# Token-shift mixes moved from VectorE to ScalarE and GpSimd, with a new table of steps, in a Mamba layer between two feed-forward blocks

## The chip, the cores and the metric

One core of one Trainium2 chip. The metric is the device time of one execution in microseconds, the median of the runs. Engines as the profile names them: PE is TensorE (PEld its weight loads), DVE is VectorE, ACT is ScalarE, POOL is GpSimd, SP is SyncE, which issues the DMAs.

## The reference

The input is 4 sequences of 2048 tokens with 512 features, fp32. Half a feed-forward block is added, then a Mamba block with its residual, then the same feed-forward block again:

```python
def ffn(x):                                     # W_r, W_k, W_v are 512 x 512, mu_r and mu_k have 512
    x_prev = concatenate([zeros, x[:, :-1]], axis=1)
    xr = mu_r * x + (1.0 - mu_r) * x_prev
    xk = mu_k * x + (1.0 - mu_k) * x_prev
    r = sigmoid(xr @ W_r.T)
    k_act = square(relu(xk @ W_k.T))
    return r * (k_act @ W_v.T)

def mamba(x):                                   # 1024 inner channels, 16 states
    xs, z = split(layernorm(x, ln_w, ln_b) @ W_in.T)
    xc = silu(b_conv + causal_conv(xs, W_conv, taps=4))
    dt_low, B, C = split(xc @ W_xproj.T)
    delta = softplus(dt_low @ W_dt.T + b_dt)
    h = exp(delta * A) * h + delta * B * xc     # a scan over the tokens
    y = (h * C).sum(states) + D_skip * xc
    return (y * silu(z)) @ W_out.T + x

x = x + 0.5 * ffn(layernorm(x))
x = x + mamba(layernorm(x))
x = x + 0.5 * ffn(layernorm(x))
```

The change is in `xr` and `xk`.

## The kernel before

The tokens are cut into 16 chunks of 512, four of each sequence in turn. Features lie on the 128 partitions for what is multiplied, tokens for what is normalised. A chunk's scan is 64 **steps**: 4 quarters of the channels (256 each, two tiles of 128) by 16 states. In each step ScalarE makes the decay (`make_decay`, lines 886 to 889: two exponentials and a zero between them), GpSimd the product of u and B (`product`, lines 1298 and 1302), VectorE scans (line 1091) and multiplies by C into g (`weigh`, line 1099), TensorE adds g up by transposing it into the accumulator y_acc (`sum_g`, line 567), ScalarE saves the last state (`save`, line 895), and SyncE loads the rows of B and C for later steps. Two decay buffers, two g buffers and four buffers of products tie the engines: ScalarE makes decay s when state s-2 is saved, which needs the multiply of step s-2; GpSimd makes product s when multiply s-4 is done.

One iteration of the loop has the 64 steps of one chunk. All other work is spread over them: the first feed-forward block and the Mamba front (input projection, convolution, x projection) of the next chunk ("front"), and the output projection and second feed-forward block of the chunk before ("back"). The step in which each piece stands is in a table of numbers written into the kernel (`TURN` to `BANK`); each engine's program goes through the 64 steps and issues in each, after its part of the scan, what the table puts there, in a fixed order of pieces. Engines run their programs in order and wait on semaphores, so a piece that waits holds up everything behind it, the decays and products of later steps too. Iterations -2 and -1 and 16 and 17 have no scan: they are the head and the tail of the program.

A feed-forward block in the order of its pieces, with the lines of the profile: ScalarE normalises rows (691), TensorE turns them (458), ScalarE copies the columns (`ffn_columns`, 708, and `ffn_lead`, 715 and 717) into `col`, which is one token longer than the chunk. Then the **mixes**: ScalarE scales the previous token by 1 - mu into `mix_k` (`ffn_before_k`, 732) and into the other mix (`ffn_before_r`, 748; it lies in `xn_col` for the first block, in `xin` for the second), and VectorE adds mu times the token itself:

```python
dve.scalar_tensor_tensor(out=mix_k[:, ct, :], in0=col[:, ct, 1:W + 1], scalar=vec[:, 1, ct:ct + 1],
                         in1=mix_k[:, ct, :], op0=ALU.mult, op1=ALU.add)      # ffn_mix_k, 1014; ffn_mix_r is 1019
```

There are 16 of these per chunk: four feature tiles, k and r, two blocks. TensorE then makes k (`ffn_k`, 472, which waits for all four k mixes), r (`ffn_r`, 483) and v (`ffn_v`, 494); ScalarE makes relu and square in `col` (756, 758) and tanh (762); VectorE gates (1026) and GpSimd adds to the residual (1287). Groups of four matmuls of 512 columns are the unit on TensorE. Others that are spoken of: the output projection (596), the x projection (531, in two halves), after which ScalarE writes `xdbl` (820), softplus with its two table loads (837, 845), the convolution (802, 1037), its silu on VectorE (1043), `make_u` (1276), and `add_zeros` (575), matmuls of a zero tile into y_acc that change nothing in it, put at the steps in `ZEROS`.

## Time and profile before

| | us |
|---|---|
| median of 3 runs | 4891.49 |
| lowest, highest | 4890.23, 4892.57 |
| span of the profiled execution | 4888.0 |
| first scan begins | 153.6 |
| last scan begins | 4779.8 |
| mean granted clock of TensorE | 0.971 |

The span is the profiled execution's own time from its first to its last instruction; the runs' median is 3.5 us longer. The program has 58,099 instructions. A busy time is the union of an engine's instructions; each instruction's time overlaps the next one's by a little, so an engine without gaps shows a step from start to start that is shorter than the sum of the durations. TensorE's matmul ends are modelled.

### The profile page before, as it was taken

The page shows a single profiled execution, that of the slowest core. Times are in us where ns is not written, and L with a number is a line of the kernel's source. Part 1 is how long each engine was busy: PE and PEld are TensorE (multiplying, and loading weights), DVE is VectorE, ACT ScalarE, POOL GpSimd, SP SyncE. Part 2 cuts the span into 40 slices and gives each one's busy share as a digit, 9 for nine tenths or more (in the row PEclk, how much of TensorE's full clock was granted, in tenths as well). Part 3 has the DMA queues.
Part 4 walks back from the last instruction along what each step waited for, and adds up shares of the span by engine and source line. Part 5 has one row for each costly group of instructions (what it writes and reads, how often), then busy time and mean ns, then how long its engine had stood idle before and what let it go on. Part 6 is the DMA issues. An engine that isn't in the chain of part 4 may idle for free.

```text
span 4888.0 us, 58099 instructions
## 1 busy us (share of the span) xinstructions
PE 4296.9 (88%) x16896; PEld 2382.9 (49%) x16896; DVE 4488.3 (92%) x3650; ACT 2900.1 (59%) x6355; POOL 3196.4 (65%) x3328
## 2 busy tenths in 40 slices
PE   6777989898999989989898899989999898999787
PEld 2444545454554545545454454545545454554443
DVE  2799999999999999999999999999999999999992
ACT  2555656666666566656666665666656666665452
POOL 1666767576676767767576676767667576776770
PEclk9888999999999999999999999999999999999798
DMA  2445555454554555555555554555555565655451
GB/s 82 141 135 180 172 171 185 163 183 162 189 169 151 189 168 186 172 173 185 158 174 163 186 172 152 190 179 176 172 185 173 155 180 156 190 170 153 167 164 62
DMA packets 423053, 810.71 MB, mean 166 GB/s; under 512 B 41264, under 2 KB 41264, under 8 KB 418640
## 3 DMA queue, kind: packets, MB, share of 16 engines
q1 hardware_dynamic: 422736, 807.00, 52.1%
q8 instruction: 136, 2.23, 0.2%
q14 instruction: 181, 1.48, 0.1%
HBM read 772.25 MB, written 34.60 MB: 165 GB/s over the span
## 4 chain that ended last, share of the span: by engine, by line
DVE 38%; PE 29%; issue 16%; ACT 7%; POOL 6%; DMA 3%; DVEq 0%; SPq 0%; POOLq 0%; ACTq 0%
DVE decay L1091 19%; DVE g L1099 10%; PE y_acc L567 6%; PE mm L494 5%; PE mm L483 5%; POOL dbx L1298 4%; PE mm L472 4%; DVE xc L1037 3%; DMA c_all<-bc_scratch 2%; PE mm L531 2%; PE mm L509 2%; PE mm L519 2%; DVE xc L1043 1%; ACT decay L889 1%; POOL xout L1287 1%
## 5 line engine op out<-in xcount | busy, mean ns | idle before, releaser
L1298 POOL TENSOR_TENSOR dbx<-u,b_all 128x1024 f32<-128x1024 f32 x1024 | 2414.2, 2358 | 902.6 <-DVE g L1099 901.7
L1091 DVE TENSOR_TENSOR_SCAN decay<-decay,state,dbx 128x1024 f32<-128x1024 f32 x1024 | 2405.4, 2349 | 172.4 <-ACT decay L889 157.6
L567 PE MATMUL y_acc<-ident,g 128*128 128x128 f32 x8192 | 1124.2, 283 | 372.5 <-DVE g L1099 370.6
L567 PEld LDWEIGHTS y_acc<-ident,g 128*128 128x128 f32 x8192 | 947.4, 144 | 939.1 <-DVE g L1099 713.2
L1099 DVE TENSOR_TENSOR g<-decay,c_all 128x1024 f32<-128x1024 f32 x1024 | 1244.3, 1215 | 10.0 <-DMA c_all<-bc_scratch 1.1
L886 ACT ACTIVATE decay<-delta,neg_a 128x512 f32<-128x512 f32 x1024 | 708.7, 692 | 36.9
L889 ACT ACTIVATE decay<-delta,neg_a 128x511 f32<-128x511 f32 x1024 | 686.9, 671 | 0.0
L895 ACT ACTIVATE state<-decay 128x2 f32<-128x2 f32 x1024 | 166.9, 163 | 508.6 <-DVE g L1099 506.1
L494 PE MATMUL mm<-wbuf_c,col 128*128 128x512 f32 x1024 | 460.9, 594 | 2.1 <-ACT col L758 1.3
L1037 DVE SCALAR_TENSOR_TENSOR xc<-mm,conv_sb,xc 128x509 f32<-128x509 f32 (+2 forms) x384 | 285.3, 743 | 47.0 <-ACT xs_last L804 35.7
L1302 POOL TENSOR_TENSOR dbx<-dbx,carry 128x1 f32<-128x1 f32 x1024 | 274.2, 268 | 80.3
L494 PEld LDWEIGHTS mm<-wbuf_c,col 128*128 128x128 f32 x1024 | 185.0, 190 | 192.0 <-issue 186.5
L802 ACT ACTIVATE xc<-mm,evec,conv_sb 128x512 f32<-128x512 f32 x128 | 99.5, 777 | 257.0 <-PE mm L509 222.9
L762 ACT ACTIVATE rows<-mm 128x512 f32<-128x512 f32 x128 | 76.2, 595 | 294.2 <-PE mm L483 294.2
L472 PE MATMUL mm<-mix_k,wbuf_c 128*128 128x512 f32 x512 | 232.7, 598 | 4.5 <-DVE mix_k L1014 4.4
L509 PE MATMUL mm<-xn_col,wbuf_d 128*128 128x512 f32 x512 | 235.2, 603 | 1.3 <-ACT xn_col L789 1.0
L483 PE MATMUL mm<-wbuf_d,xin 128*128 128x512 f32 x512 | 231.8, 596 | 4.4 <-DVE xin L1019 4.4
L596 PE MATMUL mm<-wbuf_a,gate 128*128 128x512 f32 x512 | 233.1, 598 | 2.1 <-issue 1.2
L472 PE MATMUL mm<-mix_k,wbuf_b 128*128 128x512 f32 x512 | 233.0, 599 | 1.7 <-DVE mix_k L1014 1.7
L509 PE MATMUL mm<-xn_col,wbuf_a 128*128 128x512 f32 x512 | 232.7, 598 | 1.4 <-DVE xc L1037 1.4
L519 PE MATMUL mm<-xn_col,wbuf_b 128*128 128x512 f32 x512 | 231.2, 594 | 0.0
L519 PE MATMUL mm<-xn_col,wbuf_c 128*128 128x512 f32 x512 | 230.6, 593 | 0.0
(100 smaller groups left out, 5107.4 us busy)
## 6 DMA issues: line engine op xcount, KB each, us to landing
b_all<-bc_scratch SPq DMA_DIRECT2D x1024, 256.0 KB, 3.4
c_all<-bc_scratch SPq DMA_DIRECT2D x1024, 256.0 KB, 3.6
wbuf_d<-in_w_r SPq DMA_DIRECT2D x32, 1024.0 KB, 7.5
wbuf_c<-in_w_v SPq DMA_DIRECT2D x32, 1024.0 KB, 7.3
xin<-in_x SPq DMA_DIRECT2D x16, 1024.0 KB, 6.8
wbuf_c<-in_w_k SPq DMA_DIRECT2D x16, 1024.0 KB, 6.7
wbuf_d<-in_w_in SPq DMA_DIRECT2D x16, 1024.0 KB, 5.8
wbuf_a<-in_w_in SPq DMA_DIRECT2D x16, 1024.0 KB, 8.0
```

The lines of the kernel that those rows point to most:

```text
L472: last = pe.matmul(bank(it, f"f{i}k{j}"), wk[:, ct, j * P:(j + 1) * P], mix_k[:, ct, :], start=ct == 0, stop=ct == CT - 1)
L483: last = pe.matmul(bank(it, f"f{i}r{tb}"), mix_r[:, ct, tb * P:(tb + 1) * P], wr[:, ct, :], start=ct == 0, stop=ct == CT - 1)
L494: last = pe.matmul(bank(it, f"f{i}v{tb}"), col[:, ct, tb * P:(tb + 1) * P], wv[:, ct, :], start=ct == 0, stop=ct == CT - 1)
L509: last = pe.matmul(bank(it, f"xs{e}"), win[:, ct, e % 4 * P:(e % 4 + 1) * P], xn_col[:, slot, ct, :], start=ct == 0, stop=ct == CT - 1)
L519: last = pe.matmul(bank(it, f"z{e}"), win[:, ct, e % 4 * P:(e % 4 + 1) * P], xn_col[:, slot, ct, :], start=ct == 0, stop=ct == CT - 1)
L567: last = pe.matmul(y_acc[:, tb, j * P:(j + 1) * P], g[:, s % PAIRS, j, tb * P:(tb + 1) * P], ident[:, :], start=n == 0 and j == 0 and tb % ...
L886: act.activation(d[:, 0, :], delta[:, q % 2, 0, :], ACT.Exp, scale=neg_a[:, e, n:n + 1]).then_inc(decay_done, 1)
L889: act.activation(d[:, 1, 1:W], delta[:, q % 2, 1, 1:W], ACT.Exp, scale=neg_a[:, e + 1, n:n + 1]).then_inc(decay_done, 1)
L1037: dve.scalar_tensor_tensor(out=o, in0=src[:, 0:W - late], scalar=conv_sb[:, e, q:q + 1], in1=o, op0=ALU.mult, op1=ALU.add).then_inc(m_dve. ...
L1091: dve.tensor_tensor_scan(d, d, flat(dbx[:, s % DBX, :, :]), state[:, batch, s, 0:1], ALU.mult, ALU.add).then_inc(scan_done, 1)
L1099: dve.tensor_tensor(g[:, s % PAIRS, :, :], decay[:, s % PAIRS, :, :], c_all[:, s % CRING, :].unsqueeze(1).broadcast_to([P, QT, W]), ALU.mu ...
L1298: pool.tensor_tensor(dbx[:, s % DBX, :, :], u[:, q % 2, :, :], b_all[:, s % BRING, :].unsqueeze(1).broadcast_to([P, QT, W]), ALU.mult).the ...
```

## The change

VectorE's 16 mixes per chunk are gone. ScalarE, which scaled the previous token, scales the token itself as well, by mu, into a free tile (`now`): `rows[0]` for the k mix of the first block, `rows[1]` for the r mix of the second, and `col` in place for the mix that comes last in its block. GpSimd adds the two tiles. In the second block r comes before k on ScalarE. TensorE and ScalarE wait for GpSimd's adds where they waited for VectorE's mixes, and tanh waits for an add too, since it overwrites the tile. The table of steps is new. Of its 40 or so lines these are the ones that matter here (first block or front ahead, second behind):

```diff
-        MM_K = ((5, 7, 8, 9), (46, 47, 50, 51))
+        MM_K = ((5, 7, 8, 9), (46, 48, 49, 52))
-        ZEROS = {2: 2, 31: 2, 39: 2, 30: 1, 53: 1}
+        ZEROS = {31: 1}
-        COLUMNS = ((1, 1, 2, 2), (36, 36, 36, 36))
+        COLUMNS = ((1, 2, 2, 3), (36, 36, 36, 36))
-        BEFORE_K = ((3, 3, 5, 5), (39, 39, 40, 40))
+        BEFORE_K = ((3, 3, 4, 5), (39, 39, 40, 43))
-        BEFORE_R = ((6, 7, 7, 7), (37, 37, 38, 38))
+        BEFORE_R = ((3, 5, 7, 8), (36, 37, 37, 38))
-        XROWS = 51
+        XROWS = 52
-        MIX_K = ((3, 4, 5, 5), (42, 43, 45, 46))
+        MIX_K = ((3, 4, 5, 6), (41, 42, 42, 49))
-        MIX_R = ((6, 7, 7, 8), (38, 39, 40, 40))
+        MIX_R = ((4, 6, 9, 9), (38, 39, 39, 40))
-        CSILU = (33, 34, 40, 42, 43, 45, 48, 48)
+        CSILU = (34, 36, 43, 43, 48, 48, 48, 49)
-        MAKE_U = (-8, 9, 27, 38)
+        MAKE_U = (-2, 8, 28, 37)
```

Besides, in the table: `MM_R` of the first block goes from (10, 10, 12, 13) to (10, 10, 11, 13), `XPROJ` from (49, 50) to (48, 50), `RELU` of the second block from (49, 50, 53, 53) to (49, 50, 51, 54), the loads `wxs1` from 26 to 31 and `wo0` from 48 to 51; `MM_V` is the same. Other numbers move by a step or two. The code:

```diff
@@ -203,15 +204,15 @@
                      *[(COLUMNS[i][n], f"xn{n}" + " lead last" * (n == 3)) for n in range(4)],
                      *[(RELU[i][n], f"rel{n} sq{n}") for n in range(4)],
                      *[(TANH[i][n], f"th{n}") for n in range(4)],
-                     *[(BEFORE_K[i][n], f"pk{n}") for n in range(4)],
-                     *[(BEFORE_R[i][n], f"pr{n}") for n in range(4)])) for i in range(2)]
+                     *[(q[i][n], f"p{r}{n} a{r}{n}")
+                       for q, r in ((BEFORE_K, "k"), (BEFORE_R, "r"))[::(1, -1)[i]] for n in range(4)])) for i in range(2)]
         f_dve = [Marks(sem(f"ffn{i}_dve"), in_order(
                      *[(STATS[i][n] - 64 * (2 - i), f"st{n}") for n in range(4)],
                      (MEANS[i] - 64 * (2 - i), "mv0 mv1 mv2 mv3"),
+                     *[(GATE[i][n], f"g{n}") for n in range(4)])) for i in range(2)]
+        f_pool = [Marks(sem(f"ffn{i}_pool"), ["v"] + newton + ["mean", "shift"] + in_order(
                      *[(MIX_K[i][n], f"xk{n}") for n in range(4)],
-                     *[(MIX_R[i][n], f"xr{n}") for n in range(4)],
-                     *[(GATE[i][n], f"g{n}") for n in range(4)])) for i in range(2)]
-        f_pool = [Marks(sem(f"ffn{i}_pool"), ["v"] + newton + ["mean", "shift", "o0", "o1", "o2", "o3"])
+                     *[(MIX_R[i][n], f"xr{n}") for n in range(4)]) + ["o0", "o1", "o2", "o3"])
                   for i in range(2)]
         m_pe = Marks(sem("mamba_pe"), in_order(*[(MTURN[n], f"T{n}") for n in range(4)],
                                                *[(XS[e], f"xs{e}") for e in range(ET)], (XPROJ[1], "xp")))
@@ -283,6 +284,10 @@
                 if 0 <= it + off < NCH and home(it, name) == mine:
                     return marks.sem, marks.at(it + off, emptied)
             return None
+
+        def now(i, part, ct):
+
+            return rows[i][:, ct, :] if i == part else col[:, ct, 1:W + 1]
 
         def flat(t):
             return t.rearrange("p a b -> p (a b)")
@@ -463,7 +468,7 @@
                 turn_rows(it, f"f{i}T{ct}", rows[i], ct, f_pe[i])
 
             def ffn_k(it, i, k, j):
-                pe.wait_ge(f_dve[i].sem, f_dve[i].at(k, "xk3"))
+                pe.wait_ge(f_pool[i].sem, f_pool[i].at(k, "xk3"))
                 pe.wait_ge(wk_loaded[i], 16 * (k + 1))
                 if free := bank_free(it, f"f{i}k{j}"):
                     pe.wait_ge(*free)
@@ -474,7 +479,7 @@
                 last.then_inc(f_pe[i].sem, 1)
 
             def ffn_r(it, i, k, tb, mix_r):
-                pe.wait_ge(f_dve[i].sem, f_dve[i].at(k, "xr3"))
+                pe.wait_ge(f_pool[i].sem, f_pool[i].at(k, "xr3"))
                 pe.wait_ge(wr_loaded[i], 16 * (k + 1))
                 if free := bank_free(it, f"f{i}r{tb}"):
                     pe.wait_ge(*free)
@@ -731,6 +736,12 @@
                         act.wait_ge(f_pe[1].sem, count)
                 act.activation(mix_k[:, ct, :], col[:, ct, 0:W], ACT.Copy,
                                scale=vec[:, 3, ct:ct + 1]).then_inc(f_act[i].sem, 1)
+                if i == 0:
+                    act.wait_ge(f_pe[0].sem, f_pe[0].at(k, "T3"))
+                else:
+                    act.wait_ge(f_act[1].sem, f_act[1].at(k, f"pk{ct}"))
+                act.activation(now(i, 0, ct), col[:, ct, 1:W + 1], ACT.Copy,
+                               scale=vec[:, 1, ct:ct + 1]).then_inc(f_act[i].sem, 1)
 
             def ffn_before_r(i, k, ct, mix_r, fronted=True):
 
@@ -747,11 +758,17 @@
                             act.wait_ge(f_pe[1].sem, count)
                 act.activation(mix_r[:, ct, :], col[:, ct, 0:W], ACT.Copy,
                                scale=vec[:, 2, ct:ct + 1]).then_inc(f_act[i].sem, 1)
+                if i == 1:
+                    act.wait_ge(f_pe[1].sem, f_pe[1].at(k, "T3"))
+                else:
+                    act.wait_ge(f_act[0].sem, f_act[0].at(k, f"pr{ct}"))
+                act.activation(now(i, 1, ct), col[:, ct, 1:W + 1], ACT.Copy,
+                               scale=vec[:, 0, ct:ct + 1]).then_inc(f_act[i].sem, 1)
 
             def ffn_relu2(i, k, j):
 
                 act.wait_ge(f_pe[i].sem, f_pe[i].at(k, f"k{j}"))
-                act.wait_ge(f_dve[i].sem, f_dve[i].at(k, (f"xr{j}", f"xk{j}")[i]))
+                act.wait_ge(f_pool[i].sem, f_pool[i].at(k, (f"xr{j}", f"xk{j}")[i]))
                 o = col[:, j, 0:W]
                 act.activation(o, bank(k - (1, -1)[i], f"f{i}k{j}"), ACT.Relu).then_inc(f_act[i].sem, 1)
                 act.wait_ge(f_act[i].sem, f_act[i].at(k, f"rel{j}"))
@@ -759,6 +776,7 @@
 
             def ffn_tanh(i, k, tb):
                 act.wait_ge(f_pe[i].sem, f_pe[i].at(k, f"r{tb}"))
+                act.wait_ge(f_pool[i].sem, f_pool[i].at(k, (f"xk{tb}", f"xr{tb}")[i]))
                 act.activation(rows[i][:, tb, :], bank(k - (1, -1)[i], f"f{i}r{tb}"), ACT.Tanh,
                                scale=0.5).then_inc(f_act[i].sem, 1)
 
@@ -962,10 +980,10 @@
                         for n in at(BEFORE_R[0], s):
                             ffn_before_r(0, f, n, xn_col[:, other, :, :])
                     if back:
+                        for n in at(BEFORE_R[1], s):
+                            ffn_before_r(1, b, n, xin, front)
                         for n in at(BEFORE_K[1], s):
                             ffn_before_k(1, b, n, front)
-                        for n in at(BEFORE_R[1], s):
-                            ffn_before_r(1, b, n, xin, front)
                     if front:
                         for e in at(CTANH, s):
                             conv_tanh(f, e)
@@ -1008,16 +1026,6 @@
                     dve.wait_ge(marks.sem, marks.at(k, f"st{tb}"))
                     dve.sem_inc(passed_dve, 1)
                     dve.bn_aggr(mv[q][:, tb, :], stats[q][:, tb, :]).then_inc(marks.sem, 1)
-
-            def ffn_mix_k(i, k, ct):
-                dve.wait_ge(f_act[i].sem, f_act[i].at(k, f"pk{ct}"))
-                dve.scalar_tensor_tensor(out=mix_k[:, ct, :], in0=col[:, ct, 1:W + 1], scalar=vec[:, 1, ct:ct + 1],
-                                         in1=mix_k[:, ct, :], op0=ALU.mult, op1=ALU.add).then_inc(f_dve[i].sem, 1)
-
-            def ffn_mix_r(i, k, ct, mix_r):
-                dve.wait_ge(f_act[i].sem, f_act[i].at(k, f"pr{ct}"))
-                dve.scalar_tensor_tensor(out=mix_r[:, ct, :], in0=col[:, ct, 1:W + 1], scalar=vec[:, 0, ct:ct + 1],
-                                         in1=mix_r[:, ct, :], op0=ALU.mult, op1=ALU.add).then_inc(f_dve[i].sem, 1)
 
             def ffn_gate(i, k, tb):
                 dve.wait_ge(f_pe[i].sem, f_pe[i].at(k, f"v{tb}"))
@@ -1108,16 +1116,6 @@
                     if scn:
                         scan(it, s, bt)
 
-                    if front:
-                        for n in at(MIX_K[0], s):
-                            ffn_mix_k(0, f, n)
-                        for n in at(MIX_R[0], s):
-                            ffn_mix_r(0, f, n, xn_col[:, other, :, :])
-                    if back:
-                        for n in at(MIX_K[1], s):
-                            ffn_mix_k(1, b, n)
-                        for n in at(MIX_R[1], s):
-                            ffn_mix_r(1, b, n, xin)
                     if front:
                         for e in at(CSILU, s):
                             conv_silu(f, e)
@@ -1281,6 +1279,14 @@
                 pool.tensor_tensor(carry[:, q % 2, :], carry[:, q % 2, :], state[:, batch, NS * q:NS * q + NS, 1],
                                    ALU.mult).then_inc(h_pool.sem, 1)
 
+            def ffn_mix_k(i, k, ct):
+                pool.wait_ge(f_act[i].sem, f_act[i].at(k, f"ak{ct}"))
+                pool.tensor_tensor(mix_k[:, ct, :], mix_k[:, ct, :], now(i, 0, ct), ALU.add).then_inc(f_pool[i].sem, 1)
+
+            def ffn_mix_r(i, k, ct, mix_r):
+                pool.wait_ge(f_act[i].sem, f_act[i].at(k, f"ar{ct}"))
+                pool.tensor_tensor(mix_r[:, ct, :], mix_r[:, ct, :], now(i, 1, ct), ALU.add).then_inc(f_pool[i].sem, 1)
+
             def ffn_add(i, k, tb):
                 pool.wait_ge(f_dve[i].sem, f_dve[i].at(k, f"g{tb}"))
                 o = (xin, xout)[i][:, tb, :]
@@ -1311,6 +1317,16 @@
                     if scn:
                         for q in at(MAKE_U, s):
                             make_u(it, q, bt)
+                    if front:
+                        for n in at(MIX_K[0], s):
+                            ffn_mix_k(0, f, n)
+                        for n in at(MIX_R[0], s):
+                            ffn_mix_r(0, f, n, xn_col[:, (bt + 1) % 2, :, :])
+                    if back:
+                        for n in at(MIX_K[1], s):
+                            ffn_mix_k(1, b, n)
+                        for n in at(MIX_R[1], s):
+                            ffn_mix_r(1, b, n, xin)
                     if front:
                         for n in at(FFN_ADD[0], s):
                             ffn_add(0, f, n)
```

How ScalarE's program changes in step 3 of a steady iteration (state and decay are the scan's, mix_k and xn_col the two mixes of the first block, col the columns). Before, from the state saved in step 3:

```order
L895 ACTIVATE state<-decay 128x2
L886 ACTIVATE decay<-delta,neg_a 128x512
L888 ACTIVATE decay<-zero 128x1
L889 ACTIVATE decay<-delta,neg_a 128x511
L732 ACTIVATE mix_k<-col,vec 128x512 x2
```

and now, from behind the decay of step 3 to the decay of step 4:

```order
L713 ACTIVATE col<-mm 128x512
L720 ACTIVATE col<-ffn_last0 128x4
L722 ACTIVATE ffn_last0<-col 128x4
L737 ACTIVATE mix_k<-col,vec 128x512
L743 ACTIVATE rows0<-col,vec 128x512
L737 ACTIVATE mix_k<-col,vec 128x512
L743 ACTIVATE rows0<-col,vec 128x512
L759 ACTIVATE xn_col<-col,vec 128x512
L765 ACTIVATE col<-col,vec 128x512
L913 ACTIVATE state<-decay 128x2
L904 ACTIVATE decay<-delta,neg_a 128x512
```

The last column copy and its two small ones came into step 3 from step 2, and two scaled copies have become six.

GpSimd's program in steps 3 to 6 of the same iteration (dbx are the products). Before, step after step alike:

```order
L1298 TENSOR_TENSOR dbx<-u,b_all 128x1024
L1302 TENSOR_TENSOR dbx<-dbx,carry 128x1
L1298 TENSOR_TENSOR dbx<-u,b_all 128x1024
L1302 TENSOR_TENSOR dbx<-dbx,carry 128x1
L1298 TENSOR_TENSOR dbx<-u,b_all 128x1024
```

and now:

```order
L1304 TENSOR_TENSOR dbx<-u,b_all 128x1024
L1308 TENSOR_TENSOR dbx<-dbx,carry 128x1
L1284 TENSOR_TENSOR mix_k<-mix_k,rows0 128x512
L1304 TENSOR_TENSOR dbx<-u,b_all 128x1024
L1308 TENSOR_TENSOR dbx<-dbx,carry 128x1
L1284 TENSOR_TENSOR mix_k<-mix_k,rows0 128x512
L1288 TENSOR_TENSOR xn_col<-xn_col,col 128x512
L1304 TENSOR_TENSOR dbx<-u,b_all 128x1024
L1308 TENSOR_TENSOR dbx<-dbx,carry 128x1
L1284 TENSOR_TENSOR mix_k<-mix_k,rows0 128x512
L1304 TENSOR_TENSOR dbx<-u,b_all 128x1024
L1308 TENSOR_TENSOR dbx<-dbx,carry 128x1
```

An add now stands between the products of each of these steps, and waits for ScalarE.

TensorE's program from the second k group of the second block (mix_k) to the last, with the x projection's halves (wx_sb) between. Before:

```order
L472 MATMUL mm<-mix_k,wbuf_b 128x512 x4
L567 MATMUL y_acc<-ident,g 128x128 x16
L531 MATMUL mm<-xc2,wx_sb 64x512 x4
L567 MATMUL y_acc<-ident,g 128x128 x8
L472 MATMUL mm<-mix_k,wbuf_b 128x512 x4
L531 MATMUL mm<-xc2,wx_sb 64x512 x4
L567 MATMUL y_acc<-ident,g 128x128 x8
L472 MATMUL mm<-mix_k,wbuf_b 128x512 x4
```

and now:

```order
L477 MATMUL mm<-mix_k,wbuf_b 128x512 x4
L536 MATMUL mm<-xc2,wx_sb 64x512 x4
L572 MATMUL y_acc<-ident,g 128x128 x8
L477 MATMUL mm<-mix_k,wbuf_b 128x512 x4
L572 MATMUL y_acc<-ident,g 128x128 x8
L536 MATMUL mm<-xc2,wx_sb 64x512 x4
L572 MATMUL y_acc<-ident,g 128x128 x16
L556 MATMUL y_acc<-ident,spare 128x128 x8
L477 MATMUL mm<-mix_k,wbuf_b 128x512 x4
```

Two sums of g now stand behind the second half of the x projection before the last k group; one stood there.

## Rows read from the trace of the kernel before

**Rows 1.** The page's engines: busy us (share of the span) and instructions.
```profile
PE 4296.9 (88%) x16896; PEld 2382.9 (49%) x16896; DVE 4488.3 (92%) x3650; ACT 2900.1 (59%) x6355; POOL 3196.4 (65%) x3328
```

**Rows 2.** Stretches: us; busy us (instructions) per engine; TensorE clock; DMA share, GB/s.
```profile
0.00:153.60 153.60, 93.44 (x212) 40.54 (x212) 39.64 (x70) 48.30 (x82) 27.69 (x88) 0.90 0.24 75
2191.70:2207.60 15.90, 10.43 (x64) 7.34 (x64) 15.83 (x13) 12.89 (x29) 10.55 (x8) 1.00 0.93 314
2207.60:2268.20 60.60, 59.54 (x227) 32.94 (x228) 56.67 (x40) 36.28 (x81) 42.20 (x32) 1.00 0.50 157
2351.70:2426.40 74.70, 65.03 (x244) 33.82 (x245) 74.12 (x63) 43.53 (x101) 41.81 (x35) 1.00 0.54 173
2426.40:2484.30 57.90, 53.50 (x212) 28.98 (x210) 52.95 (x46) 32.98 (x72) 43.36 (x48) 1.00 0.52 159
2191.70:2484.30 292.60, 264.00 (x1056) 145.87 (x1056) 280.31 (x230) 180.80 (x397) 199.74 (x207) 0.99 0.54 173
4527.00:4779.80 252.80, 198.28 (x834) 122.62 (x833) 240.86 (x166) 137.42 (x317) 172.55 (x148) 0.88 0.49 161
```

**Rows 3.** VectorE's timeline in steps 38 and 52: start, us, [idle before].
```profile
2363.28 0.92 DVE L1019 SCALAR_TENSOR_TENSOR xin<-col,vec,xin 128x512 f32<-128x512 f32 x1
2364.12 0.67 DVE L1048 SCALAR_TENSOR_TENSOR gate<-gate,mm 128x512 f32<-128x512 f32 x1
...
2434.51 2.36 DVE L1091 TENSOR_TENSOR_SCAN decay<-decay,state,dbx 128x1024 f32<-128x1024 f32 x1 [4.05 <-ACT decay L889]
```

**Rows 4.** Chain of waits, end of step 51: start, us, what.
```profile
2420.60 3.58 PE mm L531 x8
...
2425.20 3.44 PE mm L472 x8
2428.64 3.59 PE mm L531 x8
...
2432.25 0.69 ACT xdbl L820
...
2433.02 0.69 ACT decay L886
```

**Rows 5.** Groups by line and shape: busy us, mean ns of one, idle before.
```profile
L1014 DVE SCALAR_TENSOR_TENSOR mix_k<-col,vec,mix_k 128x512 f32<-128x512 f32 x128 | 113.2, 897 | 13.7 <-ACT mix_k L732 13.7
...
L1019 DVE SCALAR_TENSOR_TENSOR xn_col<-col,vec,xn_col 128x512 f32<-128x512 f32 x64 | 63.3, 1010 | 6.7 <-ACT xn_col L748 6.7
...
L1019 DVE SCALAR_TENSOR_TENSOR xin<-col,vec,xin 128x512 f32<-128x512 f32 x64 | 53.8, 862 | 13.6 <-ACT xin L748 13.6
...
L1287 POOL TENSOR_TENSOR xin<-xin,rows 128x512 f32<-128x512 f32 x64 | 81.4, 1271 | 167.2 <-DVE rows L1026 165.5
...
L575 PE MATMUL y_acc<-ident,zero 128*128 128x512 f32 x256 | 135.0, 643 | 0.0
```

**Rows 6.** ScalarE's timeline in steps 4 and 5.
```profile
2205.53 1.28 ACT L837 ACT_TABLE_LOAD   x1 [0.48 <-PE mm L543]
...
2209.68 0.15 ACT L895 ACTIVATE state<-decay 128x2 f32<-128x2 f32 x1
...
2211.20 1.32 ACT L732 ACTIVATE mix_k<-col,vec 128x512 f32<-128x512 f32 x2
```

**Rows 7.** TensorE's timeline in steps 2, 6, 8 and 50.
```profile
2200.71 1.88 PE L575 MATMUL y_acc<-ident,zero 128*128 128x512 f32 x4
...
2217.24 3.60 PE L472 MATMUL mm<-mix_k,wbuf_c 128*128 128x512 f32 x8
...
2227.11 1.09 PE L567 MATMUL y_acc<-ident,g 128*128 128x128 f32 x8 [0.96 <-DVE g L1099]
...
2419.51 1.09 PE L567 MATMUL y_acc<-ident,g 128*128 128x128 f32 x8 [1.31 <-DVE g L1099]
```

**Rows 8.** Durations of VectorE's k mixes and of its silus, ns min/median/max.
```profile
L1014 DVE SCALAR_TENSOR_TENSOR mix_k<-col,vec,mix_k x128: 736/910/1789, 31.2 to 4838.3; 128x512 f32<-128x512 f32 x128
...
L1043 DVE SCALAR_TENSOR_TENSOR xc<-rows,xc x128: 676/680/999, 110.8 to 4460.2; 128x512 f32<-128x512 f32 x128
```

57 lines of the change are left out of this document (29 added, 28 removed), and 6 rows, old and new, of the table BANK.

## Prediction

> **What bounds the kernel now.** I read the engines' shares first: VectorE is busy for 92% of the span, TensorE for 88% [rows 1]. Two engines are near their limit, so an average decides nothing, and I cut one steady iteration (the eighth, 292.6 us between the starts of its first scan and of the next iteration's) at the starts of steps 4, 18, 36 and 51. Head and last iteration stand beside it [rows 2]. Over the whole iteration ScalarE is busy 180.8 us and GpSimd 199.7, so neither is near. Fifteen iterations lie between 153.6 and 4527.0 us, 291.6 us each. The reader is to see two regimes. In steps 4 to 18 TensorE is busy 59.5 of 60.6 us and VectorE 56.7: TensorE sets the pace. In steps 36 to 51 VectorE is busy 74.1 of 74.7 us and TensorE 65.0: VectorE sets it [rows 2]. In steps 51 to 64 both have gaps, 4.4 us on TensorE and 5.0 on VectorE, most of the latter in one wait of 4.05 us for ScalarE's decay [rows 3]. The chain of waits tells whose wait that is: projection, up matmul, projection on TensorE back to back, then xdbl on ScalarE, then the decay queued behind it, then the scan [rows 4]. So from step 48 on the chain runs through TensorE as well.
>
> **What is removed from VectorE.** 256 mixes go: 113.2 + 63.3 + 53.8 = 230.3 us busy, 0.90 each [rows 5]. Instructions overlap a little: the mix at 2363.28 is followed at 2364.12 [rows 3], so one mix holds the engine 0.84 us. That is 13.4 us for the 16 of an iteration, of which a half belongs to each feed-forward block.
>
> The eight of the first block stand in steps 3 to 8, all but one in the stretch that TensorE bounds. Its groups (out 4 and 5, k 5 to 9, r 10 to 13, v 14 to 17) keep their steps but for one r group, moved from 12 to 11. I cost their removal at zero: the cover is 59.5 us of matmuls.
>
> The eight of the second block stand in steps 38 to 46, where VectorE has no gap. 8 x 0.84 = 6.7 us come out of each iteration. TensorE can follow: it has 65.0 us of work in 74.7, so 9.7 us of room.
>
> **What ScalarE gains.** 16 more copies with a scale per iteration. The nearest row is the scaled copy of the previous token: two in a row take 1.32 us [rows 6], so 0.66 each and 10.6 us per iteration, which 180.8 of 292.6 us leave room for. What counts is the order: the decay of step s+1 stands behind the extras of step s. Softplus with its two table loads lies in step 4, between 2205.53 and 2209.68, 4.15 us; the decay after it takes 1.52 us, to 2211.20 [rows 6]. In the changed order step 3 holds one column copy, two small copies and six scaled copies, about 5.0 us, step 4 softplus and two, 5.5 us, step 5 four, 2.6 us. Carrying this forward from the start of step 3 (decay 3 done 1.2 us after step 2's multiply, as now), decay 5 is ready some 3.4 us after VectorE, now without its mixes, would want it, decay 6 another 0.6. Part of that is time which VectorE no longer spends mixing: step 6 begins 1.6 us later than now. TensorE feels it at the sum of g of step 4, which stands ahead of the second half of an output projection and of the first up matmul, now at 2217.24; I get 2.1 us. It gets back the 0.96 us that it now waits at 2227.11 [rows 7]. That leaves +1.0 us per iteration. Bounds: zero if TensorE's queue absorbs it, 4.0 us if every late decay passes through. I take 1.0 because the queue is seen to run without a gap behind that place.
>
> In the second block ScalarE's mixes lie in steps 36 to 43. Five steps from 36 on hold 24 us for ScalarE against 23.8 for VectorE, so up to 1.1 us of stall at step 37; VectorE has 11 us more than ScalarE until step 46 and the mixes removed there still count. I take it within the 6.7 and let the range carry it.
>
> **What GpSimd gains.** 16 adds of 128x512, 1.27 us each by the adds it does already [rows 5]: 20.3 us per iteration, on an engine busy 199.7 of 292.6 [rows 2]. It runs up to four products ahead of the scan, and each add waits for ScalarE's second scale, with the next products queued behind the wait. In steps 3 to 6 this eats the lead: product 7 comes about 0.8 us before scan 7 wants it, product 9 at about the moment. I cost it at zero, covered by the late decays and the TensorE-bound stretch; without that cover it is the 0.2 to 1 us of each product. Two-input work is better left on VectorE, about twice as fast there, says the Trainium skill (GPSIMD Engine Reference, Engine selection). The rows have 1.27 against 0.90 us, and what decides is not the ratio but whose time it is.
>
> **What else moves.** Seven of the eight zero matmuls per iteration go from TensorE, 135.0 us in all now [rows 5], a pair 1.88 us [rows 7]; at steps 2, 31 and 39 TensorE waits for VectorE behind them, and I count nothing there. The x projection's last half stays at 50, xdbl goes from step 51 to 52 and up matmul 3 from 51 to 52, behind the projection. ScalarE then meets xdbl when it is done. The 4.05 us wait goes, but not as 4.05 us of time, since TensorE's own queue there has little to give: a gap of 1.31 us before the sum at 2419.51 [rows 7], and 0.9 us of the zero matmul that went from step 53. I take 2 us, bounds 0 and 4.05. The first u product of the next chunk moves from step 56 to 62, away from GpSimd's crowded step 58: nothing counted. SyncE's loads keep their weights; wxs1 goes from 26 to 31 and wo0 from 48 to 51, both ahead of their users in steps 38 and, next iteration, 5.
>
> **Head and tail.** Before the first scan no scan hides the mixes. Up matmul 0 waits for four copies and a mix; now for ten copies, as six scales of the other mix stand between, and an add: about +4.5 us. In the tail the four pairs and an add come before the first r matmul: about +3 us. Together +8.
>
> **The sum.** Per full iteration 6.7 + 2.0 - 1.0 = 7.7 us, 14 times: 108. The last iteration has the second block alone: 6.7. The first has the first block alone: -1.0. With head and tail: 4888.0 - 108 - 6.7 + 1 + 8 = 4782 us of span. The median of the runs is 3.5 us over the profiled span (4891.5 against 4888.0), so **4786 us**, 2.2% faster.
>
> **The rivals.** (A) VectorE bounds everything, and the rearrangement lets the first block's mixes count too: 15.5 x 13.4 = 208 us, less the 8: 4692 us. Against it stand 59.5 busy us in a 60.6 us stretch whose groups stay. 0.06.
>
> (B) ScalarE's and GpSimd's queues give it back. The late decays of steps 5 and 6 pass through (4 us) and steps 37 and 38 lose 3 more: 8.7 - 7 = 1.7 us per iteration, 4888 - 25 + 8 + 3.5 = 4874. For it speaks that ScalarE's work there grows from 1.3 to 5 us in one step; against it the slack behind. 0.13.
>
> (C) Slower: TensorE's clock. The zero matmuls stand in its thin places: steps 0 to 4 have 10.4 us of work in 15.9. Now the granted clock is 0.99 over the steady iteration but 0.88 in the last iteration, whose TensorE is busy 198 of 253 us, and 0.90 in the head [rows 2]. With the zeros gone, TensorE could fall to 1.2 GHz after steps 2 and 31 and carry it into steps 4 to 18, where each us at half clock costs 0.5 us. It decides from 15 us at half clock per iteration (7.7 / 0.5); with 20 the time is 4888 + 15 x 2.3 + 11.5 = 4934. Against it: shorter iterations leave TensorE busier. The Trainium skill (TensorE: Matmul & The Clock Gate, HAM oscillation) says that gaps between bursts throttle the array so that each burst begins cold; by that rule, removing filler in a thin place is the wrong way. The rows of the last iteration agree. 0.09.
>
> (D) Slower: GpSimd's adds block VectorE's silus, which read two SBUF tiles as the mixes do. A mix took up to 1.789 us against 0.736 at least; a silu 0.999 at most, 0.680 in the middle [rows 8]. If all 128 silus waited 1.05 us: 4786 + 134 = 4920. GpSimd is already at work two thirds of the time and the middle silu loses nothing. The Trainium skill (SBUF — State Buffer, Who interferes with whom) has the shared port pair as an exclusive lock held for the whole instruction, which would allow such waits. 0.02.
>
> **How the numbers follow.** The forecast has 0.70. The range, 4710 to 4872, takes in the bounds above (front 0 to 4, wait 0 to 4, silus up to 0.32 each, 41 us), some of A's gain and B nearly to its value; C and D lie outside. A measurement here tells 0.2%, 10 us, from no change. Faster by more: the forecast, A, and more than half of B, 0.84; within: 0.05; slower: C, D and a bad B, 0.11.
>
> **What would show it.** Iterations of about 284 us; VectorE busy near 4260; steps 4 to 18 still about 61 us and TensorE without gaps; steps 36 to 51 about 68; the wait before scan 52 gone or under 1 us; waits before scans 5 and 6 of 3 and 0.6 us. Steps 4 to 18 at 55 us would speak for A, at 65 for B; a granted clock under 0.95 in steps 4 to 18 for C; silus with a median over 0.9 for D.

## The result, and the profile after

| | before | changed |
|---|---|---|
| median (lowest to highest) of 4 runs, us | 4892.03 (4890.23 to 4893.06) | 4809.59 (4806.88 to 4812.95) |
| span of the profiled execution, us | 4888.0 | 4805.1 (time 4806.88) |

The ratio is 0.9832, 95% interval 0.9818 to 0.9846: 1.7% faster, where 2.2% and 4786 us were forecast. The time lies in the range, 24 us above the forecast, so the interest is in those 24 us and in whether the terms were right one by one. One execution of `a_zeros` (9082 us) and one of `a_second_both_short` (5784 us, the one that was profiled) stood far outside the others of the same kernel and are left out of every number below.

Engines and chain of waits on the page of the changed kernel (compare [rows 1]):

```profile
PE 4236.8 (88%) x16672; PEld 2383.7 (50%) x16672; DVE 4291.5 (89%) x3394; ACT 3068.6 (64%) x6611; POOL 3430.0 (71%) x3584
...
PE 50%; DVE 21%; issue 10%; POOL 7%; ACT 7%; DMA 4%; SPq 0%; DVEq 0%; POOLq 0%; ACTq 0%
```

and the chain of waits of the kernel before:

```profile
DVE 38%; PE 29%; issue 16%; ACT 7%; POOL 6%; DMA 3%; DVEq 0%; SPq 0%; POOLq 0%; ACTq 0%
```

VectorE lost 196.8 us of busy time (4488.3 to 4291.5), the span 82.9. Half of the chain that ended last is now TensorE. Stretches of the changed kernel, columns as in [rows 2]: head, steps 0 to 4, 4 to 18, 18 to 27, 36 to 51, 51 to 64 and the whole of the eighth iteration, number 7 counted from 0 (the one of [rows 2]), and the last iteration:

```profile
0.00:157.23 157.23, 93.47 (x212) 40.29 (x212) 33.90 (x62) 53.64 (x91) 36.97 (x95) 0.93 0.24 74
2158.37:2175.49 17.12, 10.99 (x58) 8.62 (x59) 15.73 (x13) 13.25 (x30) 9.95 (x9) 0.74 0.69 194
2175.49:2237.21 61.72, 61.67 (x231) 33.66 (x230) 51.73 (x34) 40.87 (x87) 50.16 (x41) 0.99 0.55 177
2237.21:2277.86 40.65, 36.95 (x153) 21.21 (x151) 37.52 (x35) 25.74 (x52) 33.53 (x47) 0.96 0.55 181
...
2319.76:2390.81 71.05, 65.70 (x243) 34.77 (x242) 69.47 (x57) 49.20 (x111) 49.74 (x44) 0.98 0.51 165
2390.81:2445.41 54.60, 49.98 (x204) 27.78 (x202) 52.26 (x43) 32.25 (x71) 41.58 (x47) 1.00 0.59 189
2158.37:2445.41 287.04, 261.67 (x1042) 147.01 (x1042) 267.96 (x213) 191.34 (x413) 214.07 (x224) 0.97 0.56 176
4444.95:4695.02 250.07, 194.02 (x816) 121.34 (x817) 235.04 (x158) 143.51 (x326) 179.51 (x156) 0.86 0.51 163
```

To compare kernels I use the means over iterations 1 to 14 of the times between the scans' starts in each trace, us; "low" is the time per iteration for which the granted clock was 0.5 (1.2 GHz):

| steps | 0-4 | 4-18 | 18-27 | 27-36 | 36-51 | 51-64 | iteration | low |
|---|---|---|---|---|---|---|---|---|
| before | 15.9 | 60.7 | 38.7 | 44.1 | 74.5 | 57.9 | 291.8 | 4.9 |
| changed | 16.9 | 61.3 | 40.4 | 41.9 | 70.8 | 54.7 | 286.0 | 13.6 |
| forecast | +1.0 for both | | 0 | 0 | -6.7 | -2.0 | 284.1 | |

So steps 0 to 18 gave back 1.6 us, steps 18 to 27 another 1.7, and steps 27 to 64 gained 9.1 against a forecast of 8.7. Iteration by iteration 5.8 us came, 81 us in 14; the first iteration gained 4.5, the last 3.2, and head and tail cost 3.6 and 1.9: 83 us in all.

VectorE's waits before scans 5 and 6 of iteration 7, forecast at 3.4 and 0.6 us (the mean over the 14 iterations is 3.4 and 0.5):

```profile
2182.93 2.36 DVE L1099 TENSOR_TENSOR_SCAN decay<-decay,state,dbx 128x1024 f32<-128x1024 f32 x1 [3.83 <-ACT decay L907]
...
2187.04 2.36 DVE L1099 TENSOR_TENSOR_SCAN decay<-decay,state,dbx 128x1024 f32<-128x1024 f32 x1 [0.50 <-ACT decay L907]
```

Groups of the changed kernel by line and shape: the silu on VectorE, ScalarE's new scale, GpSimd's adds:

```profile
L1051 DVE SCALAR_TENSOR_TENSOR xc<-rows,xc 128x512 f32<-128x512 f32 x128 | 97.4, 789 | 0.0
...
L743 ACT ACTIVATE rows<-col,vec 128x512 f32<-128x512 f32 x64 | 45.2, 707 | 0.0
...
L1288 POOL TENSOR_TENSOR xin<-xin,rows 128x512 f32<-128x512 f32 x64 | 84.9, 1337 | 76.5 <-ACT rows L765 75.8
...
L1284 POOL TENSOR_TENSOR mix_k<-mix_k,rows 128x512 f32<-128x512 f32 x64 | 81.1, 1268 | 144.7 <-ACT rows L743 144.6
```

The adds cost what the older ones do, 1.27 us [rows 5]. The silu's median is 683 ns, its longest 931, so rival D's blocked silus (a median over 0.9 us) did not come. Its mean rose from 766 to 789 ns: a silu that overlaps a GpSimd instruction takes 0.91 us and one that doesn't 0.68, in both kernels, and 79 of the 128 now overlap one where 54 did.

### The profile page after: what moved, and what is told of

The parts are those of the page before. It is cut to its first block, busy times and chain, and to the rows that moved or that the text cites. A ratio compares the mean times of both kernels' runs of the same rounds, so it can differ in the third digit from the quotient of the medians.

```text
span 4805.1 us, 58035 instructions
## 1 busy us (share of the span) xinstructions
PE 4236.8 (88%) x16672; PEld 2383.7 (50%) x16672; DVE 4291.5 (89%) x3394; ACT 3068.6 (64%) x6611; POOL 3430.0 (71%) x3584
## 4 chain that ended last, share of the span: by engine, by line
PE 50%; DVE 21%; issue 10%; POOL 7%; ACT 7%; DMA 4%; SPq 0%; DVEq 0%; POOLq 0%; ACTq 0%
PE y_acc L572 10%; DVE decay L1099 10%; PE mm L601 9%; PE mm L488 8%; PE mm L477 8%; DVE g L1107 6%; POOL dbx L1304 5%; PE mm L514 4%; DMA c_all<-bc_scratch 4%; PE mm L499 3%; DVE xc L1045 3%; PE mm L536 2%; PE mm L524 2%; PE mm L548 1%; POOL xout L1293 1%
## 5 line engine op out<-in xcount | busy, mean ns | idle before, releaser
L572 PEld LDWEIGHTS y_acc<-ident,g 128*128 128x128 f32 x8192 | 967.9, 145 | 718.0 <-DVE g L1107 424.0
L601 PE MATMUL mm<-wbuf_a,gate 128*128 128x512 f32 x512 | 248.9, 632 | 39.4 <-issue 37.4
L1308 POOL TENSOR_TENSOR dbx<-dbx,carry 128x1 f32<-128x1 f32 x1024 | 214.1, 209 | 80.3
L514 PE MATMUL mm<-xn_col,wbuf_a 128*128 128x512 f32 x512 | 251.8, 639 | 0.7 <-DVE xc L1045 0.7
L463 PE MATMUL mm<-ident,rows 128*128 128x128 f32 x768 | 121.7, 293 | 141.3 <-ACT col L713 66.3
```

Source lines behind the costliest of these rows:

```text
L514: last = pe.matmul(bank(it, f"xs{e}"), win[:, ct, e % 4 * P:(e % 4 + 1) * P], xn_col[:, slot, ct, :], start=ct == 0, stop=ct == CT - 1)
L572: last = pe.matmul(y_acc[:, tb, j * P:(j + 1) * P], g[:, s % PAIRS, j, tb * P:(tb + 1) * P], ident[:, :], start=n == 0 and j == 0 and tb % ...
L601: last = pe.matmul(bank(it, f"o{tb}"), gate[:, 4 * part + e, tb * P:(tb + 1) * P], wo[:, e, :], start=part == 0 and e == 0, stop=part == 1 ...
```

## The experiments

"b_" names an edit of the kernel before, "a_" one of the changed kernel. Each median is of three to eight runs, with the kernel before run on the same chip (4891.3 to 4893.3 us in the three sets). Of each kernel one execution was profiled.

### What a mix on VectorE is worth, block by block

`b_first_short`: VectorE's eight mixes of the first block work on one column, so that block is left without the second part of its mix; `b_second_short` does the same to the second block (`i == 1`). The k mix is shown; the r mix is cut alike.

```diff
+                n = 1 if i == 0 else W
-                dve.scalar_tensor_tensor(out=mix_k[:, ct, :], in0=col[:, ct, 1:W + 1], scalar=vec[:, 1, ct:ct + 1],
-                                         in1=mix_k[:, ct, :], op0=ALU.mult, op1=ALU.add).then_inc(f_dve[i].sem, 1)
+                dve.scalar_tensor_tensor(out=mix_k[:, ct, 0:n], in0=col[:, ct, 1:n + 1], scalar=vec[:, 1, ct:ct + 1],
+                                         in1=mix_k[:, ct, 0:n], op0=ALU.mult, op1=ALU.add).then_inc(f_dve[i].sem, 1)
```

> The kernel before, with VectorE's eight mixes of the first block cut to one column, so the token itself is left out of xr and xk there in all columns but one. VectorE has about 8 x 0.72 = 5.8 us less per iteration, ScalarE, GpSimd and the table are as before. My account (TensorE bounds steps 4 to 18): that stretch stays at 60.7 us, only the mix in step 3 counts (0.7 us), so about 4880 us. Rival A (VectorE time counts wherever it is taken out): 15 x 5.8 = 87 us less, about 4805.

> The kernel before, with VectorE's eight mixes of the second block cut to one column (left out as above). My account: steps 36 to 51 lose 5.8 us per iteration and 15 iterations have them, so 86 us less, about 4806. If it is over 4840, the 6.7 us of my sum was too large by itself and TensorE or ScalarE bounds steps 36 to 51 as soon as VectorE gives way.

Measured: 4862.35 us, ratio 0.9942 (0.9927 to 0.9957), and 4833.56 us, 0.9879 (0.9864 to 0.9893). Steps 4 to 18 of `b_first_short`:

```profile
2193.19:2252.74 59.55, 59.42 (x227) 33.10 (x228) 52.40 (x40) 36.85 (x82) 40.51 (x32) 1.00 0.47 160
```

The time fell by 31 us where 13 were forecast. VectorE lost 4.3 of its 56.7 busy us in this stretch, the stretch 1.1, and it ends at TensorE's 59.4 us of matmuls. TensorE does bound it; what the edit took from the first block's mixes was worth 1.7 us per iteration (with 0.5 in steps 0 to 4), not zero and far from all. Steps 36 to 51 of `b_second_short`, and VectorE's one-column mixes in that stretch:

```profile
2328.62:2398.84 70.22, 63.49 (x241) 33.42 (x240) 69.76 (x64) 43.20 (x101) 41.18 (x35) 1.00 0.57 184
```

```profile
L1015 DVE SCALAR_TENSOR_TENSOR mix_k<-col,vec,mix_k 128x1 f32<-128x1 f32 x4 | 1.6, 397 | 0.0
...
L1021 DVE SCALAR_TENSOR_TENSOR xin<-col,vec,xin 128x1 f32<-128x1 f32 x4 | 1.3, 333 | 0.0
```

The run fell short of the forecast 4806, but not because the price of a mix was wrong. A mix of one column still takes 0.33 to 0.40 us, so only 7.1 - 2.9 = 4.2 us left VectorE, and the stretch became 4.3 us shorter (mean of 14) with VectorE still busy 69.8 of 70.2. In this stretch each us taken from VectorE is a us of time. The 0.84 us per mix are not contradicted; what was mis-sized is the experiment, by what an instruction costs however short it is.

### What ScalarE's and GpSimd's new work costs

In the changed kernel the scale of the token itself, or the add, cut to one column in the first block, and both in the second (the mixes are so left without their second part in the block named). Of the edits the first lines of the k scale are shown:

```diff
+                n = 1 if i == 0 else W
-                act.activation(now(i, 0, ct), col[:, ct, 1:W + 1], ACT.Copy,
+                act.activation(now(i, 0, ct)[:, 0:n], col[:, ct, 1:n + 1], ACT.Copy,
```

> The changed kernel with ScalarE's new scales of the first block cut to one column (the token's own part is left out of the first block's mixes but in one column), so 8 x 0.5 = 4 us less on ScalarE per iteration and GpSimd's adds as they are. ScalarE's burst as the cause of the 1.6 us lost in steps 0 to 18: the wait before scan 5 falls from 3.9 to about 1.5 us and steps 0 to 18 come down to 76.6 to 77 us; about 4787. TensorE's work as the only bound: the wait shrinks but steps 0 to 18 stay within 0.4 us of 78.2; 4800 to 4810.

> The changed kernel with GpSimd's adds of the first block cut to one column (left out as above but for one column): 8 x 1.1 = 9 us less on GpSimd in steps 3 to 9. GpSimd's queue as the cause: waits before scans 5 and 8 shrink and steps 0 to 18 fall by over 1 us, under 4795. My prediction's account (GpSimd costs nothing): within 5 us of the changed kernel, 4805 to 4813.

> The changed kernel, second block only: ScalarE's scales of the token itself and GpSimd's adds cut to one column (15 x 8 of each); the second block's mixes are so left without their second part. If ScalarE's and GpSimd's added work costs nothing there, as predicted, steps 36 to 51 stay within 1 us of 70.8 and the time within 15 us of 4809. Rival: the queues are what kept the saving at 3.8 us where 6.7 were forecast; then the wait of 1.02 us at step 41 and the steps beside it fall away, 2 to 3 us per iteration, and the time is 4765 to 4780. The line lies at 4790.

Measured: scales 4793.71 us (4789.28 to 4805.02), 0.9803 (0.9789 to 0.9818); adds 4809.16, 0.9832 (0.9818 to 0.9847); second block 4805.34, 0.9824 (0.9808 to 0.9841), against 4809.59 for the change. The length of GpSimd's adds costs nothing that can be told, as predicted, and neither does that of either engine's new work in the second block.

Shorter scales in the first block take 16 us off the median, but the execution that was profiled is the slowest of the four (4805.02), and its iterations take 286.0 us as in the changed kernel: what the 16 us are is not seen in it. In it the wait before scan 5 falls from 3.4 to 2.7 us (means of 14), not to 1.5, and steps 0 to 18 take 77.6 us instead of 78.1. The run with shorter adds has 77.7 there at the same median as the changed kernel, so half a us in these steps tells nothing. Whether the length of the scales costs time over the whole kernel stays open (the two intervals touch at 0.9818); as the cause of the 1.6 us in steps 0 to 18 it is not borne out.

The traces show where the 1.6 us went. In steps 0 to 4 the loss is 1.0 us, and VectorE has a wait in step 2 that it did not have before. TensorE's timeline in steps 0 to 2 and VectorE's in step 2, iteration 7 of the changed kernel:

```profile
2161.72 1.06 PE L463 MATMUL mm<-ident,rows 128*128 128x128 f32 x8 [1.68 <-ACT col L713]
...
2164.72 0.63 PE L463 MATMUL mm<-ident,rows 128*128 128x128 f32 x4 [1.07 <-ACT col L713]
...
2169.37 0.69 DVE L1062 TENSOR_TENSOR gate<-gate,mm 128x512 f32<-128x512 f32 x1 [1.15 <-PE mm L590]
```

TensorE's column turns, whose banks ScalarE's copies empty, stand in another order of banks and steps than before. They wait for the copies, and VectorE's gate waits for a turn behind them. The wait is 1.1 us (mean of 14), stays at 1.0 with the zero matmuls back in place (`a_zeros`, below), and is absent in `hybrid`, which has the old turns. In steps 4 to 18 the loss is 0.6 us, and with the zero matmuls back it is gone: 60.4 us, against 60.7 before, with the wait before scan 5 still 2.6 us.

### The code without its table, and single moves of the table

`moved_only` has the changed code with the old table, and within a step r before k on ScalarE.

> The code of the change with the whole table of before: mixes moved, no step placed anew. It splits the gain. My account: the gain of the second block's mixes is there (4 to 5 us per iteration), the wait for xdbl in step 51 stays at 4 us (2 to 3 us of my sum missing), the first block costs what it does in the changed kernel: about 286 + 3 = 289 us per iteration, 4845 to 4855. If the table is what gains, it is at 4892 or above; if the table is idle, at 4810.

Measured: 4930.04 us, 1.0075 (1.0060 to 1.0090): slower than before, the side on which the table is what gains. VectorE's waits in steps 6, 8, 39 and 52:

```profile
2239.15 2.36 DVE L1098 TENSOR_TENSOR_SCAN decay<-decay,state,dbx 128x1024 f32<-128x1024 f32 x1 [2.06 <-POOL dbx L1307]
...
2249.93 2.36 DVE L1098 TENSOR_TENSOR_SCAN decay<-decay,state,dbx 128x1024 f32<-128x1024 f32 x1 [3.19 <-POOL dbx L1307]
...
2392.56 2.36 DVE L1098 TENSOR_TENSOR_SCAN decay<-decay,state,dbx 128x1024 f32<-128x1024 f32 x1 [4.94 <-ACT decay L906]
...
2457.07 2.36 DVE L1098 TENSOR_TENSOR_SCAN decay<-decay,state,dbx 128x1024 f32<-128x1024 f32 x1 [4.50 <-ACT decay L906]
```

Late adds hold up GpSimd's products, and ScalarE's longer steps hold up the decays. The longest wait, 4.94 us, goes through both: two adds stand on GpSimd ahead of a small piece of the convolution, and ScalarE waits for that with the decay queued behind:

```profile
2387.66 2.50 POOL L1287 TENSOR_TENSOR xin<-xin,rows 128x512 f32<-128x512 f32 x2
...
2390.34 0.63 ACT L828 ACTIVATE rows<-xc 128x512 f32<-128x512 f32 x1 [3.93 <-POOL xc L1267]
```

Steps 36 to 51 take 75.5 us with VectorE busy for 68.8 of them in iteration 7, 5.4 less than before [rows 2], and none of it is time. This is a loss on the slower side that my rivals had not: I had judged the new work only in the steps that the new table gives it. The table turns +39 us into -82.

`b_xdbl` takes from the table only what I credited with 2 us:

```diff
-        MM_K = ((5, 7, 8, 9), (46, 47, 50, 51))
+        MM_K = ((5, 7, 8, 9), (46, 47, 50, 52))
-        XROWS = 51
+        XROWS = 52
```

> The kernel before with the last k group of the second block moved from step 51 to 52 behind the x projection's second half, and ScalarE's copy into xdbl from step 51 to 52. Mixes and all else as they were. My term: the wait of 4.05 us before scan 52 goes and 2 us per iteration come of it, so steps 51 to 64 fall from 57.9 to 55.9 and the time is about 4861. Rival 1, TensorE's own queue holds the steps and the wait appears elsewhere: steps 51 to 64 as before, 4891. Rival 2, the whole wait is time: 53.9 and 4830. The line between mine and the rivals lies at 4876 and 4846.

Measured: 4880.03 us, 0.9974 (0.9964 to 0.9985). The iteration is 0.8 us shorter. VectorE's timeline in steps 52 to 55 of that kernel:

```profile
2426.83 1.23 DVE L1099 TENSOR_TENSOR g<-decay,c_all 128x1024 f32<-128x1024 f32 x1 [0.64 <-PE y_acc L567]
...
2433.89 2.36 DVE L1091 TENSOR_TENSOR_SCAN decay<-decay,state,dbx 128x1024 f32<-128x1024 f32 x1 [1.27 <-ACT decay L889]
...
2439.62 2.36 DVE L1091 TENSOR_TENSOR_SCAN decay<-decay,state,dbx 128x1024 f32<-128x1024 f32 x1 [1.68 <-ACT decay L889]
```

The wait of 4.05 us [rows 3] went and three of 3.6 us together came, one of them for TensorE's sum itself. Rival 1 of that run holds nearly: the order of xdbl alone frees little. In the changed kernel steps 51 to 64 fell by 3.2 us, and TensorE has 3.5 us less to do there (49.98 against 53.50 [rows 2]): before, a k group was still running for 2.2 us after step 51 had begun [rows 4]; now that work is done by then, and a zero matmul has gone. VectorE has less there too, a statistics instruction of 0.7 us that the new table puts into step 48. No run took these moves alone.

`hybrid` leaves the first block's mixes on VectorE, in their old steps, and has the changed kernel's table for the rest (the first block's turns, copies, relu and tanh and their banks are in their old places too; of the edit only the mixes are shown):

```diff
-        MIX_K = ((3, 4, 5, 6), (41, 42, 42, 49))
-        MIX_R = ((4, 6, 9, 9), (38, 39, 39, 40))
+        MIX_K = ((3, 4, 5, 5), (41, 42, 42, 49))
+        MIX_R = ((6, 7, 7, 8), (38, 39, 39, 40))
```

> The changed kernel for the second block alone; the first block's eight mixes stay on VectorE as one instruction each, with the steps of before for its columns, mixes, relu and tanh. My account: steps 0 to 18 take 76.6 us as before, since VectorE's time is free there, steps 36 to 64 the 125.6 of the changed kernel, the head is that of before: 14 x 6.8 + 3 us less, about 4794, some 16 us under the changed kernel. Rival A: VectorE has 6.7 us more per iteration than in the changed kernel, so it is slower than that by up to 100 us, about 4900.

Measured: 4813.84 us, 0.9837 (0.9822 to 0.9852), a miss. Against the full change head and first iteration gained 10 us, but the iteration took 287.0 us and steps 4 to 18 61.8. In step 6 a mix ran beside a product of GpSimd; the timeline:

```profile
2182.08 2.36 POOL L1318 TENSOR_TENSOR dbx<-u,b_all 128x1024 f32<-128x1024 f32 x1
2183.05 1.94 DVE L1036 SCALAR_TENSOR_TENSOR xn_col<-col,vec,xn_col 128x512 f32<-128x512 f32 x1
```

1.94 us where mixes of this tile took 1.01 on average [rows 5]. Such meetings stood in the kernel before too, only at other mixes: the eight mixes of the first block take 8.1 us in `hybrid` and 7.5 before (means of 14). That is 0.6 of the 1.1 us that steps 4 to 18 lost against before; what makes the rest is not shown.

### Two entries of the table that were priced at nothing

Seven of the eight zero matmuls went (`ZEROS`), and softplus of the third quarter moved from step 19 to 20 (`DELTA`), which the prediction did not name. A 2 x 2 of the two, everything else as in the changed kernel:

```diff
-        ZEROS = {31: 1}
+        ZEROS = {2: 2, 31: 2, 39: 2, 30: 1, 53: 1}
-        DELTA = (-10, 4, 20, 34)
+        DELTA = (-10, 4, 19, 34)
```

> The changed kernel with the zero matmuls of before at their five steps. It separates the two causes for the 1 to 2 us that steps 0 to 18 got longer. ScalarE's burst in steps 3 to 5: nothing comes back, the time is 4805 to 4815 and the waits before scans 5 and 6 stay at 3.9 and 0.5 us. Rival C, the clock: the half clock of 7 to 10 us in steps 4 to 18 goes back to 0 to 3 us, the stretch to 60.7 us and the time falls by 14 x 1 or more, to under 4796.

> The changed kernel with the third quarter's softplus back in step 19 (DELTA 20 to 19). In the changed kernel TensorE sits 2.6 us before the first output projection of step 19, whose bank softplus has to empty, and steps 18 to 27 are 1.7 us longer than before. My account now: that stretch returns to 38.7 to 39 us and the time falls by 14 x 1.5 = 21 us or so, to about 4789. If the wait is only filled by another (VectorE or a later wait bounds steps 18 to 36), the sum of steps 18 to 36 stays at 82.3 us and the time at 4806 to 4813.

> The changed kernel with two entries of the table set back: the zero matmuls as before (8 per iteration) and softplus of the third quarter in step 19. Alone, the zeros took 0.9 us out of steps 4 to 18 and cost 1.5 in steps 18 to 27, where TensorE then waited for the bank that softplus empties; alone, step 19 gave back 1.8 us in steps 18 to 27 and lost 1.6 in steps 36 to 42, with TensorE at half clock. If the two losses are what the other entry mends, both gains stay: 2.5 us per iteration, about 4774, iterations near 283.5. Rival: what is taken from one stretch is given to the next whichever entry is changed, because TensorE's work per iteration is the bound: iterations of 285.5 to 286, 4800 to 4812.

| us (ratio, 95%) | softplus in 20 | softplus in 19 |
|---|---|---|
| without zeros | 4809.59 (0.9818 to 0.9846) | 4806.80 (0.9812 to 0.9845) |
| with zeros | 4813.38 (0.9805 to 0.9844) | **4770.56** (0.9736 to 0.9769) |

Alone, the zeros were to bring the time under 4796 us if the clock is the cause, and the softplus to 4789; both missed, and either does nothing that can be told. Together they were to give about 4774, and they give 39 us, and the result beats both kernels: 2.5% faster than before. The reason for softplus first. TensorE's timeline in step 19 of the changed kernel:

```profile
2241.92 1.09 PE L572 MATMUL y_acc<-ident,g 128*128 128x128 f32 x8
2245.59 5.06 PE L601 MATMUL mm<-wbuf_a,gate 128*128 128x512 f32 x8 [2.58 <-issue]
```

The output projection waits 2.58 us, and starts when the first half of softplus on ScalarE has emptied its bank. It runs its first part at the low clock, 5.06 us where a group takes 3.60 [rows 7]. In `a_delta19`, with softplus a step earlier, gap and slow group are both gone. VectorE pays 3.10 us in step 23. With zeros but softplus in 20 the same gap is there and the group takes longer:

```profile
2247.13 6.61 PE L601 MATMUL mm<-wbuf_a,gate 128*128 128x512 f32 x8 [2.58 <-issue]
```

so that steps 18 to 27 take 41.9 us and, with the 0.7 us that zeros cost in steps 27 to 36, eat what they bring elsewhere. With softplus in 19 they take 38.6, as before the change. Then the clock is what is left. Iterations 3 and 4 of `a_delta19`, each whole and with its steps 36 to 42:

```profile
1014.61:1301.73 287.12, 264.34 (x1042) 149.21 (x1042) 268.09 (x213) 191.38 (x413) 213.93 (x224) 0.96 0.55 176
...
1173.95:1206.47 32.52, 28.28 (x101) 16.14 (x99) 29.40 (x27) 23.21 (x51) 24.05 (x23) 0.86 0.49 165
...
1301.73:1584.63 282.90, 257.15 (x1044) 143.77 (x1042) 267.92 (x214) 191.17 (x413) 214.33 (x224) 0.99 0.55 179
...
1458.95:1489.38 30.43, 25.96 (x98) 13.86 (x96) 29.26 (x27) 22.87 (x51) 24.36 (x23) 0.94 0.55 175
```

One program, one execution, neighbouring iterations: 23.9 us at the low clock and 287.1 us, or 3.4 us and 282.9. 12.5 of the 15.4 us at the low clock (means of 14) fall into steps 0 to 4 and 36 to 42, where zeros had stood. TensorE in steps 39 to 41 of iteration 7 of `a_delta19`:

```profile
2331.23 0.63 PE L590 MATMUL mm<-ident,y_rows 128*128 128x128 f32 x4 [1.41 <-DVE gate L1062]
2334.49 1.97 PE L572 MATMUL y_acc<-ident,g 128*128 128x128 f32 x8 [2.63 <-DVE g L1107]
2336.26 5.59 PE L514 MATMUL mm<-xn_col,wbuf_a 128*128 128x512 f32 x8
```

and of `a_zeros_delta19`, with that whole iteration:

```profile
2319.79 1.88 PE L580 MATMUL y_acc<-ident,zero 128*128 128x512 f32 x4
2322.59 1.09 PE L572 MATMUL y_acc<-ident,g 128*128 128x128 f32 x8 [0.91 <-DVE g L1107]
2323.51 3.60 PE L514 MATMUL mm<-xn_col,wbuf_a 128*128 128x512 f32 x8
```

```profile
2143.95:2426.99 283.04, 264.41 (x1058) 147.99 (x1056) 267.84 (x213) 191.57 (x413) 214.11 (x224) 0.99 0.55 179
```

1.88 us of matmuls that change nothing fill a gap of 2.63 us, and the group behind runs in 3.60 us instead of 5.59. Over the iteration the zeros bring the low time from 15.4 to 6.3 us and the iteration from 285.55 to 283.25.

`hybrid_delta19` is `hybrid` with softplus in 19.

> The second block's mixes on ScalarE and GpSimd, the first block's on VectorE at their old steps, and softplus of the third quarter in step 19. Without step 19 this form took 4813.8, with a head 7 us and a first iteration 3 us shorter than the full change and iterations of 287.0. If step 19 gives 2.4 us in steps 18 to 27 and nothing is lost behind it: iterations of 284.6, 4780. Rival, as in the full change the gain goes again in steps 36 to 42: 4800 to 4814.

Measured: 4816.48 us, 0.9844 (0.9829 to 0.9858): the rival. Steps 18 to 27 gained 2.4 us and steps 36 to 51 lost them (71.2 to 73.6), with 10.0 us at the low clock there instead of 4.4. The same trade without zeros, once more.

## Why the prediction was right, and where not

**The second block's 6.7 us: right in size, hidden by a move.** Steps 36 to 51 fell by 3.7 us. VectorE's busy time there fell by 4.7 (74.1 to 69.5), not by 6.7, because a silu and a statistics instruction (1.7 us together) moved in from the stretches beside it; it now idles 1.6 us where it idled 0.6, 1.0 of it at a convolution in step 41 that waits for ScalarE. What moved had left other stretches: steps 27 to 36 fell by 2.2 us, which I had at nothing. There a silu (0.9 us in that stretch) and a statistics instruction (0.7) are gone, and 0.7 us comes back when the zero matmuls do (42.6 us in `a_zeros` against 41.9). I cut by stretch and took the table's moves of VectorE's work as free.

**The wait before scan 52: 2 us, wrong in mechanism.** Steps 51 to 64 fell by 3.2 us, and 2.6 us of VectorE's idle time went from them, but `b_xdbl` shows that the order of xdbl alone gives 0.8. That the forecast lies near is luck: moves of TensorE's and VectorE's work over the cut at step 51, which I had not priced, stand where the order of xdbl did in my sum.

**The first block at zero: nearly.** `b_first_short` gives 1.7 us; in the change none of it is left.

**ScalarE's burst, +1.0 us: the 1.6 us that came are not the burst.** The two waits came as forecast, 3.8 and 0.5 us against 3.4 and 0.6. But 1.0 of the 1.6 us lies in steps 0 to 4, ahead of the burst, and goes with VectorE's wait for TensorE's turns in step 2. The 0.6 us in steps 4 to 18 goes with the low clock (0.74 granted in steps 0 to 4 of iteration 7 against 1.00 [rows 2]): with the zeros back these steps take 60.4 us, so the burst costs nothing in them, the lower bound of its term. That 1.0 was near to what came is luck.

**GpSimd at zero: right** in the steps that the new table gives the adds, shown twice; with the old table they held up products and decays (`moved_only`). The 1.27 us of an add against the 0.90 of a mix compares two kinds of instruction; of one kind and size (tensor_tensor, 128x1024) GpSimd's product takes 2.36 us and VectorE's multiply into g 1.22 (means of the kernel before), and there the factor is nearly two.

**"At steps 2, 31 and 39 TensorE waits for VectorE behind them, and I count nothing there": the step that failed.** Behind a gap the clock is low and the next group slow. This is rival C's mechanism at about half its price: 15.4 against 6.3 us at the low clock cost 2.3 us per iteration, 0.25 us for each and not 0.5, after the 0.8 us that the zeros themselves cost in steps 27 to 36 (42.7 against 41.9). One kernel alone shows much the same: 20.5 us more at the low clock made an iteration of `a_delta19` 4.2 us longer, 0.2 us for each. I take it that part of TensorE's time has slack; no run shows that by itself. C as a forecast (slower than before) did not come; its mechanism did, at 36 us (4806.80 against 4770.56).

The Trainium skill (TensorE: Matmul & The Clock Gate, HAM oscillation) says that bursts behind gaps begin cold; these rows agree in direction.

**Softplus in step 20: not named at all.** It costs 43 us where zeros stand (4813.38 against 4770.56), and where they don't 3, which can't be told from nothing.

**Head, tail and ends.** +8 forecast, +5.5 measured; the first iteration gained 4.5 us where a loss of 1.0 stood, the last 3.2 where 6.7 stood. Why is open.

The sum of 284.1 us per iteration is nearly met once the two entries are mended (283.2 us), but not by its own terms: steps 36 to 51 then gain 4.4 us of the 6.7, steps 51 to 64 3.2 where 2.0 stood, steps 27 to 36 1.4 where nothing stood, and steps 0 to 18 lose 0.6 of the 1.0. 286.0 - 283.2 = 2.8 us per iteration, 39 us in 14, is what the two entries cost the change as it is. Rivals A and B fall: steps 4 to 18 take 61.3 us, neither 55 nor 65. How the low clock of steps 0 to 4 divides between the missing zeros and the new order of turns is only bounded, since no run changed the turns alone: 2.7 us per iteration before, 2.0 with zeros and the new turns (`a_zeros`), 3.4 without zeros and with the old ones (`hybrid`), 6.1 in the changed kernel.

## What to carry to other kernels

A us taken from an engine is a us of time only where that engine is busy all through; cut the iteration into stretches first, and follow each instruction that a new schedule moves over a cut, on the bounding engine above all. A forecast that comes true can still owe its size to terms that cancel, so check it stretch by stretch. Two losses can cover each other: setting either entry back alone looked like nothing, both gave 39 us, so undo suspected parts in pairs before calling them free. Filler in a thin place of TensorE was worth its cost here, with real matmuls right behind it, once the long wait elsewhere was gone.

## What was not expected of the hardware

- A mix of one column on VectorE takes 0.33 to 0.40 us (means in steps 36 to 51) beside 0.87 to 0.94 for 512 columns in the same steps: cutting an instruction's size to measure its cost leaves two fifths of it. Part of that is GpSimd: alone a mix of one column takes 0.22 us (`b_first_short`).
- A mix of 512 columns takes 0.74 us alone and 0.91 (medians of the kernel before) when it overlaps a GpSimd instruction, at worst 2.11. VectorE's multiply into g, which has two SBUF inputs too, takes 1.21 us either way. It works the other way too: GpSimd's add of one column (`dbx<-dbx,carry`) takes 0.52 us beside a mix or a silu and 0.19 otherwise; its mean before and now:

```profile
L1302 POOL TENSOR_TENSOR dbx<-dbx,carry 128x1 f32<-128x1 f32 x1024 | 274.2, 268 | 80.3
```

```profile
L1308 POOL TENSOR_TENSOR dbx<-dbx,carry 128x1 f32<-128x1 f32 x1024 | 214.1, 209 | 80.3
```

- In the kernels here the first iteration ran 84 to 99 us at the low clock (before: 91.9), later ones 0 to 24, and neighbouring iterations of one program differed by 4 us with it.
